# Layer norm scaling of a two-layer transformer-like kernel: two of four tiles moved from VectorE to GpSimd

## The chip, the cores and the metric

One NeuronCore of a Trainium2 chip runs the whole program in one launch. The time is device microseconds from the start to the end of an execution. The engines are TensorE (PE, matmuls and transposes), VectorE (DVE), ScalarE (ACT), GpSimd (POOL) and SyncE (SP, which only issues DMAs). Each works through its own queue strictly in order, and they meet at semaphores.

## What is computed

The input is x, 8 sequences of 1024 tokens with 256 features, in float32. Six blocks follow each other, each on a layer norm of x and each added back to x:

```python
x = x + 0.5 * L0_ffn(layernorm(x))    # token-shift mix, gate, squared relu, sigmoid
x = x + L0_attn(layernorm(x))         # linear attention, 16 heads of 16, chunked
x = x + 0.5 * L0_ffn(layernorm(x))
x = x + 0.5 * L1_ffn(layernorm(x))    # dense layer + one of four low-rank experts per token
x = x + L1_attn(layernorm(x))         # causal softmax attention with rotary embedding
x = x + 0.5 * L1_ffn(layernorm(x))

def layernorm(x):
    m, v = mean(x), var(x)            # over the 256 features
    return (x - m) / sqrt(v + 1e-5)
```

## The kernel before

The kernel is written engine by engine, with its own semaphores and no scheduler. A batch (one sequence) is cut into two halves of 512 tokens, and a half into four tiles of 128 tokens; a tile is 128 partitions by 256 features. The first five blocks of a half up to the rotated queries and keys are the front stream (`front_*`, halves 0 and 1). The softmax attention of all batches is the core stream (`core_*`: scores for the row maxima, L750; scores transposed, L765; exponent on ScalarE, L1310; causal select on GpSimd, L1458; values, L784). The output projection and the last block are the tail stream (`tail_*`, q = 2 and 3).

`weave` sets the order of the work. It counts 1166 ticks. In each tick every engine's code takes one step of the core stream and one step of each live generator, and a `yield` ends a step. The front of batch b starts at tick 120 b + 4 (half 0) and 120 b + 26 (half 1). Four engines run the same ticks; only VectorE's core stream lags by one. So the order on an engine is fixed by where the yields stand, and there is no clock: an engine that is held lets its whole queue wait.

Each norm has the same steps, and q tells half and stream:

- VectorE, tick 0: `bn_stats` (L819) and `bn_aggr` (L822), four each, into `mv`; semaphore `ln`.
- GpSimd, tick 1: variance plus epsilon (L1327), then to the power -0.5 (L1329) into `rstd`; semaphore `rs`.
- VectorE, tick 2: four `tensor_scalar` (L828), one per tile, (x - mean) * rstd into the buffer `dst`; semaphore `xn`.
- TensorE, tick 3: waits for four counts of `xn`, then eight transposes (L497) into two banks.
- ScalarE, tick 4: copies them to `xnT` (L1129), which the block's matmuls read.

There are 96 such norms: 5 x 2 x 8 in the front, 2 x 8 in the tail. The next batch's input overwrites x only when `xn` has reached 20 per batch, i.e. when all five norms of a half have been scaled.

GpSimd's other work stands in the same queue: the causal selects (L1458, 512), the shifted mix of the first block (L1341), the heads spread for linear attention (L1361), values by the key norm (L1369), masks (L1376), state sums (L1389), the rotary sum (L1432), and the router's root (L1413, L1415). On VectorE the core stream has the row maxima (L1104 with a mask, L1107 without), which free the two score banks that L750 fills.

Of the kernel before, what the change touches and what calls it, by code (L numbers as in the profile page):

```python
# [12 lines left out]
ALU = mybir.AluOpType  # L13
# [11 lines left out]
NC = T // CH  # L25
# [31 lines left out]
def macaron(nc, a, out):  # L57
    ctx = ExitStack()
    with ctx:
# [41 lines left out]
        mv = sb("mv", [P, 2 * NC, 4, 2])  # L101
# [318 lines left out]
        def idle(n):  # L420
            for _ in range(n):
                yield

        if True:

            with nc.Block() as block:
# [38 lines left out]
                def xq(q):  # L465
                    return x[:, 4 * q:4 * q + 4] if q < NC else xt[:, q - NC]
# [348 lines left out]
                def ln_dve(q, b, n, dst, ready):  # L815
                    xs = xq(q)
                    ready()
                    for t in range(4):
                        nc.vector.bn_stats(stats[:, q, t], xs[:, t]).then_inc(s["ln"][q], 1)  # L819
                    nc.vector.wait_ge(s["ln"][q], 8 * norms(q, b, n) + 4)  # L820
                    for t in range(4):
                        nc.vector.bn_aggr(mv[:, q, t], stats[:, q, t]).then_inc(s["ln"][q], 1)  # L822
                    yield
                    yield
                    nc.vector.wait_ge(s["ln"][q], 8 * norms(q, b, n) + 8)
                    nc.vector.wait_ge(s["rs"][q], 2 * norms(q, b, n) + 2)
                    for t in range(4):
                        nc.vector.tensor_scalar(dst[:, t], xs[:, t], mv[:, q, t, 0:1], rstd[:, q, t:t + 1], ALU.subtract,  # L828
                                                ALU.mult).then_inc(s["xn"][q], 1)
                    yield  # L830
                    yield
                    yield
# [488 lines left out]

                def ln_pool(q, b, n):
                    yield
                    nc.gpsimd.wait_ge(s["ln"][q], 8 * norms(q, b, n) + 8)
                    nc.gpsimd.tensor_scalar(varep[:, q], mv[:, q, :, 1], EPS, None, ALU.add).then_inc(s["rs"][q], 1)  # L1327
                    nc.gpsimd.wait_ge(s["rs"][q], 2 * norms(q, b, n) + 1)
                    nc.gpsimd.tensor_tensor(rstd[:, q], varep[:, q], mhalf[:], ALU.pow).then_inc(s["rs"][q], 1)  # L1329
                    yield  # L1330
                    yield from idle(3)

                def ffn_pool(c, b, f):
                    yield from ln_pool(c, b, 2 * f)
                    xT_ready(nc.gpsimd, c, b, 2 * f)
                    if b and f == 0 and c == 0:
                        nc.gpsimd.wait_ge(s["vout"][1], 16 * b)
                    if c:
                        nc.gpsimd.wait_ge(s["carry"], 2 * b + f + 1)
                    for k in range(KT):  # L1340
                        nc.gpsimd.tensor_scalar(xmB[:, :, k], xnT[c][:, k, PAD - 1:PAD - 1 + CH].rearrange("p (h t) -> p h t", h=2),  # L1341
                                                mu[:, 1, 1, k:k + 1], zcol[:], ALU.mult, ALU.add).then_inc(s["mixr"][c], 1)
                    yield
                    yield from idle(8)

                def lin_pool(c, b):
                    yield from ln_pool(c, b, 1)
                    if c == 0:
                        nc.gpsimd.memset(vlin[:, :, :, DK:2 * DK], 0.0).then_inc(s["lz"], 1)
                    yield from idle(7)  # L1350

                    def spread_heads(j):
                        if c == 0 and j == 0 and b >= 3:
                            f_filled(nc.gpsimd, 3, b - 3, "up", 1)
                        if j == 0:
                            for m in range(KT):
                                f_gone(nc.gpsimd, c, b, "q", m)
                        if j >= 2:
                            f_filled(nc.gpsimd, c, b, "sc", j - 2, 3)
                        for o in range(2):  # L1360
                            nc.gpsimd.tensor_scalar(qbd[:, j % 2, :, o], qT[:, :, j * P:(j + 1) * P], pmask[:, o:o + 1], zcol[:],  # L1361
                                                    ALU.mult, ALU.add).then_inc(s["qbd"][c], 1)

                    def scaled(j):
                        if j == 0:
                            nc.gpsimd.wait_ge(s["newton"][c], NEWTON * b + NEWTON)
                        f_gone(nc.gpsimd, c, b, "kv", j)
                        v = vlin[:, j].rearrange("p q (s d) -> p q s d", d=DK)[:, :, 0:3:2]
                        nc.gpsimd.tensor_tensor(v, v, krs[:, j].rearrange("p (q s) -> p q s", s=2).unsqueeze(3).broadcast_to([P, H // 2, 2, DK]),  # L1369
                                                ALU.mult).then_inc(s["vs"][c], 1)  # L1370

                    def select(j):
                        for i in (2, 3):
                            f_gone(nc.gpsimd, c, b, "sc", j, i)
                            v = scm[:, i].rearrange("p (j c) -> p j c", j=G)
                            nc.gpsimd.affine_select(out=v, in_=v, compare_op=ALU.is_ge, fill=0.0, base=0, pattern=[[0, G], [1, P]],  # L1376
                                                    channel_multiplier=-1).then_inc(s["sel"][c], 1)

                    def state(j):
                        t = 4 * c + j  # L1380
                        if t == 0 or t == NT - 1:
                            return
                        f_gone(nc.gpsimd, c, b, "st", j)
                        if t >= 2:
                            nc.gpsimd.wait_ge(s["st"], 6 * b + t - 1)
                            f_filled(nc.gpsimd, (t - 1) // 4, b, "y", (t - 1) % 4)
                        else:
                            f_gone(nc.gpsimd, 0, b, "st", 0)
                        nc.gpsimd.tensor_tensor(ssb[:, t % 2], ssb[:, (t - 1) % 2], smask, ALU.add).then_inc(s["st"], 1)  # L1389

                    spread_heads(0)
                    yield
                    spread_heads(1)
                    yield
                    for j in range(4):
                        if j == 0:
                            for i in range(4):
                                scaled(i)
                        if j in (1, 2):
                            spread_heads(j + 1)  # L1400
                        yield
                        yield
                        select(j)
                        state(j)
                        yield
                    yield from idle(4)

                def exp_pool(q, b, n):
                    e = 1 if q == 3 else 0
                    yield from ln_pool(q, b, n)  # L1410
                    yield from idle(4)
                    nc.gpsimd.wait_ge(s["es"][q], 17 * b + 3)
                    nc.gpsimd.tensor_scalar(narrow[:, e, 0], narrow[:, e, 0], 1e-24, None, ALU.max).then_inc(s["ep"][q], 1)  # L1413
                    nc.gpsimd.wait_ge(s["ep"][q], 2 * b + 1)
                    nc.gpsimd.tensor_tensor(narrow[:, e, 1], narrow[:, e, 0], mhalf[:], ALU.pow).then_inc(s["ep"][q], 1)  # L1415
                    yield
                    yield from idle(8)

                def qkv_pool(c, b):
                    yield from ln_pool(c, b, 4)  # L1420
                    yield
                    if c == 0:
                        nc.gpsimd.wait_ge(s["xu"][1], 4 * b + 4)
                        nc.gpsimd.memset(vst[:, :, :, DK:VP], 1.0).then_inc(s["vone"][0], 1)
                    yield
                    yield

                    def add(qk):
                        nc.gpsimd.wait_ge(s["rab"][c], 4 * b + 2 * qk + 2)
                        for m in range(KT):  # L1430
                            f_gone(nc.gpsimd, c, b, "qk", qk, m)
                        nc.gpsimd.tensor_tensor(ra, ra, rb, ALU.add).then_inc(s["rr"][c], 1)  # L1432

                    add(0)
                    yield
                    yield from idle(3)
                    add(1)
                    yield
                    yield from idle(2)
# [163 lines left out]
```

## Time and profile before

| | us |
|---|---|
| median of 3 runs | 2963.05 |
| lowest, highest | 2957.84, 2965.12 |
| the profiled execution | 2963.63 |
| its span | 2961.9 |

The span runs from the first to the last instruction of the profiled execution; its own time holds another 1.7 us around it. Busy time doesn't count instructions that only wait or issue DMAs. A timeline row gives start, length, engine, line and how many instructions are merged in it; in brackets is the idle time ahead of it and what ended that. `arena` is the name of one large buffer in which many tiles lie; `bank` is PSUM.

### The profile page before, as it was taken

Reading aid. Unit: us, or ns where it says so; the run is one execution under the profiler, and the core shown is the slowest. Engines: PE = TensorE matmul, PEld = TensorE weight load, DVE = VectorE, ACT = ScalarE, POOL = GpSimd, SP = SyncE. Lnnn points to the kernel's source line nnn. Section 1 sums busy time; section 2 is a strip of 40 time slices with the busy share of each in tenths; the row PEclk is TensorE's granted clock in tenths of the full one; section 3 lists DMA queues with packets and bytes.
Section 4 is the critical chain, followed back from the end, with each engine's and each line's share of the span. In section 5 each row is a group of like instructions: output and inputs, shape, how many; then the busy total and the mean of one; then the engine's idle time right before and its main releaser. Section 6 shows DMA issues by size and latency. Waiting matters only on the chain.

```text
span 2961.9 us, 45503 instructions
## 1 busy us (share of the span) xinstructions
PE 2640.6 (89%) x15278; PEld 1740.0 (59%) x15278; DVE 1862.2 (63%) x5534; ACT 1230.0 (42%) x2802; POOL 754.6 (25%) x1283
## 2 busy tenths in 40 slices
PE   4885899899999999899999999989998999998986
PEld 3563666456655666466665666556664666555644
DVE  5544667666677567666667666675676666766642
ACT  1321244444444444444444444444444444444452
POOL 2321232223222232223322232222322233211111
PEclk8996899989999999999999899999999999999998
DMA  2015103411333113411134113331134121443211
GB/s 59 1 46 134 23 17 80 115 41 25 70 91 98 39 41 82 129 49 45 38 96 123 40 27 68 93 95 45 35 78 123 52 52 23 100 119 76 64 38 47
DMA packets 137423, 193.97 MB, mean 65 GB/s; under 512 B 49439, under 2 KB 111214, under 8 KB 127854
## 3 DMA queue, kind: packets, MB, share of 16 engines
q1 hardware_dynamic: 131808, 190.89, 25.9%
q8 instruction: 129, 2.11, 0.3%
q10 hardware_dynamic: 5390, 0.18, 0.1%
q14 instruction: 96, 0.79, 0.1%
HBM read 122.34 MB, written 67.63 MB: 64 GB/s over the span
## 4 chain that ended last, share of the span: by engine, by line
PE 71%; DVE 16%; DMA 4%; issue 3%; ACT 3%; POOL 2%; SPq 1%; DVEq 0%; ACTq 0%; POOLq 0%
PE bank L765 9%; PE bank L784 9%; PE bank L750 8%; PE bank L587 5%; PE bank L678 4%; PE bank L518 4%; PE bank L567 4%; PE bank L527 3%; PE bank L536 3%; PE bank L692 3%; DVE bank L1104 3%; PE bank L622 2%; PE bank L497 2%; PE bank L633 2%; PE bank L561 2%
## 5 line engine op out<-in xcount | busy, mean ns | idle before, releaser
L1310 ACT ACTIVATE pexp<-bank 128x512 f32<-128x512 f32 (+3 forms) x1536 | 675.8, 497 | 555.1 <-PE bank L765 554.9
L1104 DVE CUSTOM_DVE_ANT_0 bank<-bank,maskneg 128x256 f32<-128x256 f32 (+3 forms) x1024 | 484.9, 511 | 294.1 <-PE bank L750 291.5
L765 PE MATMUL bank<-stq,stk 128*128 128x512 f32 (+3 forms) x1536 | 558.6, 435 | 58.0 <-ACT pexp L1310 54.9
L750 PE MATMUL bank<-stk,stq 128*128 128x512 f32 (+3 forms) x1536 | 512.8, 399 | 100.1 <-DMA stk<-k_halves 31.3
L765 PEld LDWEIGHTS bank<-stq,stk 128*128 128x128 f32 x1536 | 274.5, 200 | 344.3 <-ACT pexp L1310 210.4
L1107 DVE TENSOR_REDUCE mxa<-bank 128x1 f32<-128x512 f32 x512 | 348.7, 685 | 133.2 <-PE bank L750 128.4
L1458 POOL TENSOR_SCALAR_AFFINE_SELECT pexp<-pexp 128x256 f32<-128x256 f32 x512 | 214.3, 425 | 743.0 <-ACT pexp L1310 742.6
L750 PEld LDWEIGHTS bank<-stk,stq 128*128 128x128 f32 x1536 | 288.2, 203 | 184.5 <-issue 120.6
L784 PE MATMUL bank<-pexp,vsm 128*32 128x512 f32 (+3 forms) x3072 | 360.9, 544 | 5.7 <-POOL pexp L1458 5.5
L1376 POOL TENSOR_SCALAR_AFFINE_SELECT arena<-arena 128x512 f32<-128x512 f32 x128 | 78.5, 638 | 416.3 <-ACT arena L1212 416.3
L587 PE MATMUL bank<-arena 32*128 32x256 f32 x1024 | 158.0, 428 | 17.2 <-DVE arena L911 14.2
L1327 POOL TENSOR_SCALAR varep<-mv 128x4 f32<-128x4 f32 x96 | 22.6, 235 | 488.6 <-DVE mv L822 488.6
L1129 ACT COPY xnT<-bank 128x512 f32<-128x512 f32 x160 | 88.8, 602 | 140.3 <-PE bank L497 140.1
L518 PE MATMUL bank<-arena,wk 128*128 128x256 f32 x512 | 141.0, 425 | 6.5 <-DVE arena L852 6.4
L497 PE MATMUL bank<-ident,arena 128*128 128x128 f32 x768 | 119.4, 306 | 30.7 <-DVE arena L828 29.9
L587 PEld LDWEIGHTS bank<-arena 32*128 32x128 f32 x1024 | 95.2, 198 | 69.8 <-issue 51.7
L497 PEld LDWEIGHTS bank<-ident,arena 128*128 128x128 f32 x768 | 101.3, 159 | 54.5 <-DVE arena L828 34.7
L1432 POOL TENSOR_TENSOR arena<-arena 128x1024 f32<-128x1024 f32 x32 | 75.8, 2368 | 224.1 <-DVE arena L1026 224.1
L784 PEld LDWEIGHTS bank<-pexp,vsm 128*32 128x32 f32 x3072 | 63.5, 112 | 117.5 <-issue 89.8
L911 DVE TENSOR_TENSOR arena<-bank,mask 128x512 f32<-128x512 f32 x128 | 82.2, 683 | 77.0 <-PE bank L587 77.0
L518 PEld LDWEIGHTS bank<-arena,wk 128*128 128x128 f32 x512 | 108.3, 217 | 37.5 <-DVE arena L852 10.8
L1150 ACT ACTIVATE arena<-bank 128x512 f32<-128x512 f32 x64 | 38.3, 598 | 207.0 <-PE bank L518 207.0
(186 smaller groups left out, 4204.3 us busy)
## 6 DMA issues: line engine op xcount, KB each, us to landing
stq<-q_halves SPq DMA_DIRECT2D x128, 256.0 KB
arena<-rope_table SPq DMA_DIRECT2D x8, 2048.0 KB
q_halves<-arena SPq DMA_DIRECT2D x32, 512.0 KB, 3.0
k_halves<-arena SPq DMA_DIRECT2D x32, 512.0 KB, 2.8
stk<-k_halves SPq DMA_DIRECT2D x64, 256.0 KB
stk<-k_halves SPq DMA_DIRECT2D x128, 128.0 KB
v_rows<-arena SPq DMA_DIRECT2D x16, 544.0 KB, 4.1
vsm<-v_rows SPq DMA_DIRECT2D x16, 544.0 KB, 3.8
```

Of the source, the lines that this page charges most:

```text
L497: last = nc.tensor.transpose(bk[:, t * P:(t + 1) * P], src[:, t, k * P:(k + 1) * P], ident[:])
L518: last = mm(bk[:, m * D:(m + 1) * D], wk0[:, k, m * P:(m + 1) * P], xmA[:, h, k], start=k == 0, stop=k == KT - 1)
L567: last = mm(bk, xn[:, k, j * P:(j + 1) * P], wqkv[:, k, D:3 * D], start=k == 0, stop=k == KT - 1)
L587: last = mm(bks[i][:, k * D:(k + 1) * D], khT[rows, k, j * P:(j + 1) * P], qbd[rows, j % 2, k], start=k == 0, stop=k == KT - 1, skip_group ...
L678: mm(bk[:, i * D:(i + 1) * D], xn[:, k, t * P:(t + 1) * P], wf1[:, k], start=k == 0, stop=False)
L750: last = mm(bk[:, col:col + n], stq[b_][:, h % 2, qb * P:(qb + 1) * P], stk[b_][:, h % 2, k0:k0 + n], start=True, stop=True)
L765: mm(ps(j)[:, 0:n], stk[b_][:, j, kb * P:(kb + 1) * P], stq[b_][:, j, (c + 1) * CH - n:(c + 1) * CH], start=True, stop=True).then_inc(s["t ...
L784: last = mm(ps(2)[HP * j:HP * (j + 1), CH - n:CH], vsm[:, kb, at:at + HP], pexp[:, (u - 1 + j // 2) % NPX, j % 2, 0:n], start=kb == 0, sto ...
L1104: last = nc.vector.tensor_tensor_reduce(out=sc, in0=sc, in1=maskneg[:, CH - n:CH], scale=1.0, scalar=LOWEST, op0=ALU.add, op1=ALU.max, acc ...
L1107: last = nc.vector.reduce_max(dst, sc, AX)
L1310: nc.scalar.activation(pexp[:, u % NPX, j, 0:n], ps(j)[:, 0:n], ACT.Exp, scale=DK ** -0.5).then_inc(s["exp_done"], 1)
L1458: nc.gpsimd.affine_select(out=v, in_=v, compare_op=ALU.is_ge, fill=0.0, base=0, pattern=[[0, 2], [1, P]], channel_multiplier=-1).then_inc( ...
```

## The change

In `ln_dve` VectorE scales tiles 0 and 1 only. In `ln_pool` GpSimd, which has just computed the root, takes the next tick's step too. It waits for its own root (`rs`) and for the first count of `xn` of this norm, that is, for the end of VectorE's scaling of tile 0, and then scales tiles 2 and 3 into the same buffer with the same operands. Each scaling still adds one to `xn`, so that TensorE waits for the same four counts. The callers pass the buffer.

```diff
--- before.py
+++ after.py
@@ -824,7 +824,7 @@
                     yield
                     nc.vector.wait_ge(s["ln"][q], 8 * norms(q, b, n) + 8)
                     nc.vector.wait_ge(s["rs"][q], 2 * norms(q, b, n) + 2)
-                    for t in range(4):
+                    for t in range(2):
                         nc.vector.tensor_scalar(dst[:, t], xs[:, t], mv[:, q, t, 0:1], rstd[:, q, t:t + 1], ALU.subtract,
                                                 ALU.mult).then_inc(s["xn"][q], 1)
                     yield
@@ -1321,17 +1321,23 @@
 
 
 
-                def ln_pool(q, b, n):
+                def ln_pool(q, b, n, dst):
+                    xs = xq(q)
                     yield
                     nc.gpsimd.wait_ge(s["ln"][q], 8 * norms(q, b, n) + 8)
                     nc.gpsimd.tensor_scalar(varep[:, q], mv[:, q, :, 1], EPS, None, ALU.add).then_inc(s["rs"][q], 1)
                     nc.gpsimd.wait_ge(s["rs"][q], 2 * norms(q, b, n) + 1)
                     nc.gpsimd.tensor_tensor(rstd[:, q], varep[:, q], mhalf[:], ALU.pow).then_inc(s["rs"][q], 1)
                     yield
+                    nc.gpsimd.wait_ge(s["rs"][q], 2 * norms(q, b, n) + 2)
+                    nc.gpsimd.wait_ge(s["xn"][q], 4 * norms(q, b, n) + 1)
+                    for t in (2, 3):
+                        nc.gpsimd.tensor_scalar(dst[:, t], xs[:, t], mv[:, q, t, 0:1], rstd[:, q, t:t + 1], ALU.subtract,
+                                                ALU.mult).then_inc(s["xn"][q], 1)
                     yield from idle(3)
 
                 def ffn_pool(c, b, f):
-                    yield from ln_pool(c, b, 2 * f)
+                    yield from ln_pool(c, b, 2 * f, xns)
                     xT_ready(nc.gpsimd, c, b, 2 * f)
                     if b and f == 0 and c == 0:
                         nc.gpsimd.wait_ge(s["vout"][1], 16 * b)
@@ -1344,7 +1350,7 @@
                     yield from idle(8)
 
                 def lin_pool(c, b):
-                    yield from ln_pool(c, b, 1)
+                    yield from ln_pool(c, b, 1, xns)
                     if c == 0:
                         nc.gpsimd.memset(vlin[:, :, :, DK:2 * DK], 0.0).then_inc(s["lz"], 1)
                     yield from idle(7)
@@ -1407,7 +1413,7 @@
 
                 def exp_pool(q, b, n):
                     e = 1 if q == 3 else 0
-                    yield from ln_pool(q, b, n)
+                    yield from ln_pool(q, b, n, xns if q < NC else xnsG[q - NC])
                     yield from idle(4)
                     nc.gpsimd.wait_ge(s["es"][q], 17 * b + 3)
                     nc.gpsimd.tensor_scalar(narrow[:, e, 0], narrow[:, e, 0], 1e-24, None, ALU.max).then_inc(s["ep"][q], 1)
@@ -1417,7 +1423,7 @@
                     yield from idle(8)
 
                 def qkv_pool(c, b):
-                    yield from ln_pool(c, b, 4)
+                    yield from ln_pool(c, b, 4, xnsq)
                     yield
                     if c == 0:
                         nc.gpsimd.wait_ge(s["xu"][1], 4 * b + 4)
```

(Lines of GpSimd behind the edit stand six higher in the changed kernel: L1458 becomes L1464.)

VectorE's queue keeps its order. It is shown where two norms stand close together, which is some 1280 us into the program, where both halves' tail norms follow each other. Before:

```order
L1104 ISA mxb 128x1
L828 TENSOR_SCALAR arena<-arena,mv,rstd 128x256 x4
L819 BN_STATS stats<-arena 128x6 x4
L822 BN_AGGR mv<-stats 128x2 x4
L1104 ISA bank,mxa<-bank,maskneg 128x128
```

Now:

```order
L1104 ISA mxb 128x1
L828 TENSOR_SCALAR arena<-arena,mv,rstd 128x256 x2
L819 BN_STATS stats<-arena 128x6 x4
L822 BN_AGGR mv<-stats 128x2 x4
L1104 ISA bank,mxa<-bank,maskneg 128x128
```

Only the count of L828 differs, there and in the other 95 norms.

GpSimd's queue at the same place, over both norms. The roots are L1327 and L1329 (now L1328 and L1330), the causal selects L1458 (now L1464), the router's root L1413 (now L1419). Before:

```order
L1327 TENSOR_SCALAR varep<-mv 128x4
L1329 TENSOR_TENSOR rstd<-varep,mhalf 128x4
L1458 AFFINE_SELECT pexp<-pexp 128x2x128
L1327 TENSOR_SCALAR varep<-mv 128x4
L1329 TENSOR_TENSOR rstd<-varep,mhalf 128x4
L1458 AFFINE_SELECT pexp<-pexp 128x2x128 x5
L1413 TENSOR_SCALAR narrow<-narrow 128x4
```

Now:

```order
L1328 TENSOR_SCALAR varep<-mv 128x4
L1330 TENSOR_TENSOR rstd<-varep,mhalf 128x4
L1335 TENSOR_SCALAR arena<-arena,mv,rstd 128x256 x2
L1464 AFFINE_SELECT pexp<-pexp 128x2x128
L1328 TENSOR_SCALAR varep<-mv 128x4
L1330 TENSOR_TENSOR rstd<-varep,mhalf 128x4
L1464 AFFINE_SELECT pexp<-pexp 128x2x128
L1335 TENSOR_SCALAR arena<-arena,mv,rstd 128x256 x2
L1464 AFFINE_SELECT pexp<-pexp 128x2x128 x4
L1419 TENSOR_SCALAR narrow<-narrow 128x4
```

The new pair L1335 stands directly behind the root in the first norm, ahead of a select that followed the root before; in the second norm one of the five selects comes between.

## Rows read from the trace of the kernel before

**Rows 1.** The page: busy time of each engine, and the chain by engine.
```profile
PE 2640.6 (89%) x15278; PEld 1740.0 (59%) x15278; DVE 1862.2 (63%) x5534; ACT 1230.0 (42%) x2802; POOL 754.6 (25%) x1283
...
PE 71%; DVE 16%; DMA 4%; issue 3%; ACT 3%; POOL 2%; SPq 1%; DVEq 0%; ACTq 0%; POOLq 0%
```

**Rows 2.** Windows of start, steady part and end: engines, clock, DMA.
```profile
core 0: us, PE busy (x) PEld busy (x) DVE busy (x) ACT busy (x) POOL busy (x), PEclk, DMA share, GB/s
...
372.00:2560.00 2188.00, 2041.18 (x12098) 1346.45 (x12091) 1443.32 (x4317) 969.89 (x2220) 585.80 (x995) 0.95 0.27 66
```

**Rows 3.** Waits of TensorE: who waited for whom, total, times, longest.
```profile
PE bank L497 <- DVE arena L828: 29.9, 11, 6.8
PE bank L750 <- DVE mxa L1104: 29.9, 30, 2.3
...
PE bank L784 <- POOL pexp L1458: 5.5, 8, 0.7
```

**Rows 4.** Groups by line and shape on VectorE and GpSimd.
```profile
L828 DVE TENSOR_SCALAR arena<-x,mv,rstd 128x256 f32<-128x256 f32 x320 | 116.6, 426 | 8.7 <-POOL rstd L1329 8.4
...
L828 DVE TENSOR_SCALAR arena<-arena,mv,rstd 128x256 f32<-128x256 f32 x64 | 23.3, 424 | 6.4 <-POOL rstd L1329 6.4
...
L1361 POOL TENSOR_SCALAR arena<-arena,pmask,zcol 128x256 f32<-128x256 f32 x128 | 72.5, 577 | 54.4 <-PE bank L679 48.9 <-ACT arena L1183 5.5
L1369 POOL TENSOR_TENSOR arena<-arena,krs 128x256 f32<-128x256 f32 x64 | 52.9, 857 | 28.8 <-DVE krs L884 28.8
```

**Rows 5.** Timeline of the first norm (start, us, engine, what).
```profile
39.15 1.05 POOL L1329 TENSOR_TENSOR rstd<-varep,mhalf 128x4 f32<-128x4 f32 x1
40.30 1.38 DVE L828 TENSOR_SCALAR arena<-x,mv,rstd 128x256 f32<-128x256 f32 x4 [1.57 <-POOL rstd L1329]
...
41.74 1.97 PE L497 MATMUL bank<-ident,arena 128*128 128x128 f32 x8 [6.84 <-DVE arena L828]
```

**Rows 6.** Timeline: two norms close together, 1275 to 1287 us.
```profile
1275.66 0.68 POOL L1458 TENSOR_SCALAR_AFFINE_SELECT pexp<-pexp 128x256 f32<-128x256 f32 x1
...
1279.94 1.37 DVE L828 TENSOR_SCALAR arena<-arena,mv,rstd 128x256 f32<-128x256 f32 x4
...
1281.34 0.43 PE L784 MATMUL bank<-pexp,vsm 128*32 128x128 f32 x8
...
1281.70 1.09 PE L497 MATMUL bank<-ident,arena 128*128 128x128 f32 x8
...
1284.61 1.55 DVE L828 TENSOR_SCALAR arena<-arena,mv,rstd 128x256 f32<-128x256 f32 x4 [0.80 <-POOL rstd L1329]
...
1286.08 0.68 DVE L1104 CUSTOM_DVE_ANT_0 bank<-bank,maskneg 128x512 f32<-128x512 f32 x1
...
1286.97 0.47 PE L750 MATMUL bank<-stk,stq 128*128 128x512 f32 x1 [1.28 <-DVE mxa L1104]
```

**Rows 7.** Timeline: norms before router work and 1.49 us before transposes.
```profile
1134.03 1.50 DVE L828 TENSOR_SCALAR arena<-x,mv,rstd 128x256 f32<-128x256 f32 x4
...
1137.03 1.27 PE L497 MATMUL bank<-ident,arena 128*128 128x128 f32 x5
...
1305.45 1.47 DVE L828 TENSOR_SCALAR arena<-x,mv,rstd 128x256 f32<-128x256 f32 x4
...
1306.97 1.97 PE L497 MATMUL bank<-ident,arena 128*128 128x128 f32 x8 [0.47 <-DVE arena L828]
...
1311.77 0.99 PE L765 MATMUL bank<-stq,stk 128*128 128x512 f32 x2 [0.56 <-ACT pexp L1310]
```

**Rows 8.** Timeline: first and last stalls behind a scaling and VectorE work.
```profile
331.06 0.47 PE L750 MATMUL bank<-stk,stq 128*128 128x512 f32 x1 [1.23 <-DVE mxa L1104]
...
2668.59 0.47 PE L750 MATMUL bank<-stk,stq 128*128 128x512 f32 x1 [2.27 <-DVE mxa L1104]
```

**Rows 9.** Timeline: GpSimd's two-pointer scale alone, and over L828.
```profile
1012.71 1.10 POOL L1361 TENSOR_SCALAR arena<-arena,pmask,zcol 128x256 f32<-128x256 f32 x2
...
1065.38 1.30 POOL L1361 TENSOR_SCALAR arena<-arena,pmask,zcol 128x256 f32<-128x256 f32 x2
```

## The prediction

> **What bounds the kernel now.** I read the page first, for the load of the engines and for the chain of work that ended last. TensorE is busy 89% of the span and carries 71% of the chain; VectorE is busy 63% and carries 16%; GpSimd is busy 25% and carries 2% [rows 1]. The windows then show that the long middle, 372 to 2560 us, has TensorE at 2041 of 2188 us, with a granted clock of 0.95 [rows 2]. So the kernel is near the limit of one engine. A change elsewhere can win only those waits of TensorE that its engine ends, and lose only where it makes new ones.
>
> The view of TensorE's waits names them. It waited 29.9 us in 11 places for a scaling (L828) itself, and 29.9 us in its score matmuls for the maximum on VectorE (L1104), whose bank was not free; for GpSimd's causal select (L1458) it waited 5.5 us in all [rows 3]. The two VectorE waits pull this change in opposite directions. The first wants the four scaled tiles soon. The second wants VectorE free soon.
>
> **The change, part by part.** VectorE loses two of four L828 in each of 96 norms: 192 of 384 instructions, whose groups hold 116.6 + 23.3 us of busy time [rows 4]. Four together took 1.38 us on a quiet engine [rows 5], at about 0.41 us for one and a start every 0.32 us; two take 0.73. VectorE is thus free 0.65 us earlier, 96 times, or 62 us in all (3% of its busy time). Its statistics and the root on GpSimd are not touched.
>
> GpSimd gains 192 scalings. No row shows one there. The nearest is L1361: the same kind of instruction, two per-partition operands, 256 elements, one input from SBUF. Two of them took 1.10 us alone and 1.30 us while a scaling ran on VectorE [rows 9]. From below I take two at 0.41 each as VectorE does them, 0.8 us. From above I take L1369, 256 elements from two tensors, 857 ns each [rows 4], so 1.7 us. I use 1.2 us, between the two readings of L1361, because VectorE's second scaling will overlap the start of GpSimd's first.
>
> **When the four tiles are ready.** GpSimd waits until VectorE's first scaling has ended. In the first norm the root ended at 40.20 and VectorE started at 40.30 [rows 5], so a wait across engines costs 0.1 us. The new end is 0.41 + 0.1 + 1.2 = 1.71 us after VectorE's start, where it was 1.38: 0.33 us later (bounds: 0.07 earlier at 0.8 us a pair, 0.83 later at 1.7). I set the end of the fourth scaling against the first transpose for all 96 norms. In 16 the transpose starts within 0.2 us: the eleven waits of [rows 3] and five near them, mostly at the start (40.30, then 41.74, [rows 5]) and at the end, and one per batch as at 1305.45, then 1306.97 [rows 7]. There the delay is paid: 16 x 0.33 = **5.3 us lost**. One more per batch has 0.38 us of slack (1279.94 + 1.37, then 1281.70, [rows 6]) and just covers it. The other norms of the steady part have more than half a microsecond, most of them more than one (1134.03 + 1.50, then 1137.03, [rows 7]).
>
> **What VectorE's relief is worth.** I followed the chain in stretches of 60 us and looked at what stands behind each L828 on it. In 24 places more VectorE work comes first and then a wait of TensorE, the first at 331.06 (apart from one in the start-up) with 1.23 us, the last but one at 2668.59 with 2.27 us [rows 8]. These waits sum to about 25 us, but each can shrink only by 0.65 us, or twice that where two norms follow each other, or by all of itself. That gives some 18 us. Five of the pairs look like [rows 6]: L828 at 1279.94, statistics, root, L828 at 1284.61, L1104 at 1286.08, TensorE after 1.28 us of waiting at 1286.97. The same five and one near the end lose something on the other side, below: about 5 us. That leaves 13 us. TensorE arrives earlier at its next wait and gives some of it back, since 147 us of the steady window are still idle [rows 2]; I take three quarters, **10 us won**.
>
> **What stands behind the new wait on GpSimd.** It works in order. Today it finishes the root and goes on to the next selects while VectorE is still microseconds away from its scaling (the select at 1275.66, the scaling at 1279.94, [rows 6]); now it stops there. Behind the waiting instruction stand the causal selects, which TensorE's value matmuls (L784) wait for. For each select I compared its new start (old start, or the end of GpSimd's pair) with the L784 that needs it: 59 needed ones are late, by 0.4 to 7.7 us, but nearly all have more slack than that. Six do not. Five are of the kind in [rows 6]: the select that ran at 1275.66 is now held until the pair is done at 1281.6, ends at 1282.0, and the L784 that stood at 1281.34 starts some 0.75 us late. The sixth costs 1.5. This is the 5 us already taken off. The root of a following norm never comes late: at 1283 GpSimd has been free for a microsecond. Selects, masks and head spreads that VectorE, ScalarE or TensorE need otherwise are held by less than their slack.
>
> A rule that speaks against the change: VectorE's scaling reads one tensor, yet four of them took 1.55 us beside selects at 1284.61 and 1.37 us without [rows 6], and GpSimd's pair 1.30 instead of 1.10 [rows 9]. So the two engines do hold each other up. The Trainium skill (SBUF — State Buffer, Who interferes with whom) has them share one pair of ports as an exclusive lock, and exempts a one-input VectorE instruction outside its two-port modes; the lock is borne out here, the exemption isn't. With a full lock GpSimd's first scaling would start only when VectorE's second has ended, at 0.73 us rather than 0.51, and the loss at the 16 transposes would be 16 x 0.45 = 7 us in place of 5.3.
>
> **The sum.** 2963.6 (this execution) + 5.3 - 10 = 2959. The median of the runs shown is 0.6 us below the profiled execution, so 2958.5.
>
> **Rivals.** What a measurement of this kernel can tell from no change is about 0.3%, or 9 us.
>
> (a) Forecast: loss and gain nearly cancel, 2954 to 2972 us. For it: 93% of the steady part is matmul time that nothing here touches, and both terms are small. Chance 0.54.
>
> (b) The relief goes through in full. 18 us come off, the late selects cost nothing because TensorE itself arrives later there, and stalls behind other VectorE work shrink too. 2963 - 18 + 5 = 2950, perhaps 2944. For it: VectorE has 16% of the chain [rows 1]. Against it: VectorE's queue runs dry often, and where it does, being early is worth nothing. Chance 0.27.
>
> (c) Slower: GpSimd's scaling is dear. The place is the transposes. At 0.857 us each (L1369's price) the tiles are 0.83 us late: 16 x 0.83 = 13.3 at the tight transposes, 5 x 0.45 = 2.2 at those with 0.38 us of slack, 6 x 0.6 = 3.6 more for late selects, against the 10 won: 2963 + 19 - 10 = 2972. From a pair of 1.7 us upwards it decides; at 2.2 us, where norms with 1.3 us of slack come in as well, it is 2985 or more. Against it: L1361 at 577 ns in the mean of 128, busy VectorE included [rows 4]. Chance 0.19, which includes a queue on GpSimd that jams more often than my comparison says. The Trainium skill (GPSIMD Engine Reference, Key points) says that "for elementwise work, the DVE is structurally ~2× faster", that is some 0.8 us for one scaling; its table in Engine selection calls one-input work roughly line-rate, and L1361 sides with that.
>
> **Range.** Low 2943 takes in (b). High 2976 takes in the threshold case of (c); beyond it I leave 0.08, below it 0.06. The likeliest case by itself is 2954 to 2972. Chances: faster by over 0.3% 0.27, within it 0.54, slower 0.19.
>
> **What would show it.** L828 at 192 instructions, 0.73 us a pair, and near 70 us busy. The new GpSimd line at 0.56 to 0.65 us each, near 115 us busy, so GpSimd at 29%. TensorE's wait for scaling (now on GpSimd) up from 29.9 us by about 5; its waits on L1104 and L1107 down by about 10; its wait on the select up from 5.5 to some 10. TensorE's busy time is unchanged within 2 us at the same clock. I am wrong if the new line takes over 0.8 us, if TensorE waits for selects more than 15 us, or if the waits on the score maxima fall by 20 us.

## The result, and the profile after

| | before | after |
|---|---|---|
| median, us | 2964.09 (4 runs) | 2999.16 (4 runs) |
| lowest, highest | 2957.84, 2968.92 | 2984.51, 3001.8 |
| the profiled execution | 2963.63 | 3001.8 |

The ratio is 1.0109 with an interval of 1.0071 to 1.0147. The changed kernel is 35 us slower, and the time lies outside the predicted 2943 to 2976. The cause had a place among the rivals, as (c), but the price was far beyond the one that I worked with.

The page of the changed kernel, busy time and the chain by engine:

```profile
PE 2646.7 (88%) x15278; PEld 1746.7 (58%) x15278; DVE 1800.0 (60%) x5342; ACT 1232.6 (41%) x2802; POOL 980.8 (33%) x1475
...
PE 58%; DVE 11%; POOL 3%; issue 3%; DMA 2%; ACT 2%; SPq 1%; DVEq 0%; POOLq 0%; ACTq 0%
```

VectorE lost 62 us, as computed [rows 1]. GpSimd gained 226 us, where I had put 115. TensorE's busy time rose by 6.1 us and the span by 38.1, so 32 us of the rise are time in which TensorE isn't busy. The shares of the two chains can't be compared: before they add up to 100% of the span, here to 80%, since this one is followed back only to some 600 us. The waits of TensorE say where the idle time is:

```profile
PE bank L497 <- POOL arena L1335: 65.4, 32, 8.5
...
PE bank L750 <- DVE mxa L1107: 25.9, 29, 3.1
...
PE bank L587 <- DVE arena L911: 20.9, 20, 3.2
PE bank L784 <- POOL pexp L1464: 19.2, 14, 3.3
PE bank L750 <- DVE mxa L1104: 15.8, 20, 1.4
PE bank L750 <- DVE mxb L1104: 14.9, 31, 2.1
```

Three of these rows of the kernel before, beside those in [rows 3]:

```profile
PE bank L750 <- DVE mxa L1107: 25.7, 29, 2.8
...
PE bank L587 <- DVE arena L911: 14.2, 14, 2.6
...
PE bank L750 <- DVE mxb L1104: 11.2, 29, 1.2
```

The wait for scalings went from 29.9 to 65.4 us and that for selects from 5.5 to 19.2; the linear attention's masked scores (L911) cost 6.7 us more. The score matmuls wait for the row maxima in three rows, which fell together from 66.8 to 56.6 us, so by the 10 us that were predicted. The largest of them alone (29.9 to 15.8) would say more than that. The groups by line and shape on both engines name the reason:

```profile
L1335 POOL TENSOR_SCALAR arena<-x,mv,rstd 128x256 f32<-128x256 f32 x160 | 196.3, 1233 | 197.1 <-DVE arena L828 197.1
L1335 POOL TENSOR_SCALAR arena<-arena,mv,rstd 128x256 f32<-128x256 f32 x32 | 39.2, 1233 | 32.6 <-DVE arena L828 32.6
...
L828 DVE TENSOR_SCALAR arena<-x,mv,rstd 128x256 f32<-128x256 f32 x160 | 58.5, 408 | 7.8 <-POOL rstd L1330 7.6
```

One scaling on GpSimd takes 1233 ns. I had taken 600 for half a pair, and 850 as the upper bound. The 230 us behind the second bar, over 96 norms, are GpSimd idle until VectorE's first scaling has ended, with its own queue held up behind it. The timeline of the first norm, to be laid beside [rows 5]:

```profile
39.22 1.05 POOL L1330 TENSOR_TENSOR rstd<-varep,mhalf 128x4 f32<-128x4 f32 x1
40.38 0.73 DVE L828 TENSOR_SCALAR arena<-x,mv,rstd 128x256 f32<-128x256 f32 x2 [1.57 <-POOL rstd L1330]
40.98 2.45 POOL L1335 TENSOR_SCALAR arena<-x,mv,rstd 128x256 f32<-128x256 f32 x2 [0.71 <-DVE arena L828]
...
43.49 1.33 PE L497 MATMUL bank<-ident,arena 128*128 128x128 f32 x5 [8.52 <-POOL arena L1335]
```

Everything around the pair is nearly as computed: VectorE's two take 0.73 us, and GpSimd starts 0.60 us behind VectorE, where 0.51 was computed. But the pair takes 2.45 us, so the tiles are ready 3.05 us behind VectorE's start instead of 1.38. In all 96 norms it is 3.03 to 3.09 us. I set the end of the pair against the transpose again: now 38 norms are tight (within 0.2 us), where 16 were before. The eleventh norm's transposes, in the changed kernel:

```profile
302.25 1.97 PE L497 MATMUL bank<-ident,arena 128*128 128x128 f32 x8 [2.05 <-POOL arena L1335]
```

and the same ones in the kernel before:

```profile
285.97 1.97 PE L497 MATMUL bank<-ident,arena 128*128 128x128 f32 x8 [0.38 <-DVE arena L828]
```

That is 16.3 us of delay within the first 300 us, where one stream runs alone and nothing lies behind a norm to fill the gap. At the 34th norm (962 us) it is 24.6 us behind, at the 58th (1648 us) 31.4, at the last (2935 us) 35.9.

### The profile page after: what moved, and what is told of

Same layout as the page of the kernel before. It is cut to its first block, busy times and chain, and to the rows that moved or that the text cites. A ratio compares the mean times of both kernels' runs of the same rounds, so it can differ in the third digit from the quotient of the medians.

```text
span 3000.0 us, 45599 instructions
## 1 busy us (share of the span) xinstructions
PE 2646.7 (88%) x15278; PEld 1746.7 (58%) x15278; DVE 1800.0 (60%) x5342; ACT 1232.6 (41%) x2802; POOL 980.8 (33%) x1475
## 4 chain that ended last, share of the span: by engine, by line
PE 58%; DVE 11%; POOL 3%; issue 3%; DMA 2%; ACT 2%; SPq 1%; DVEq 0%; POOLq 0%; ACTq 0%
PE bank L765 8%; PE bank L784 8%; PE bank L750 6%; PE bank L678 3%; PE bank L587 3%; PE bank L527 3%; PE bank L567 3%; PE bank L536 3%; PE bank L692 2%; PE bank L497 2%; PE bank L518 2%; DVE bank L1104 2%; POOL arena L1335 2%; PE bank L679 2%; PE bank L622 2%
## 5 line engine op out<-in xcount | busy, mean ns | idle before, releaser
L1464 POOL TENSOR_SCALAR_AFFINE_SELECT pexp<-pexp 128x256 f32<-128x256 f32 x512 | 209.9, 416 | 629.4 <-ACT pexp L1310 628.8
L784 PE MATMUL bank<-pexp,vsm 128*32 128x512 f32 (+3 forms) x3072 | 359.7, 543 | 19.5 <-POOL pexp L1464 19.2
L1335 POOL TENSOR_SCALAR arena<-x,mv,rstd 128x256 f32<-128x256 f32 x160 | 196.3, 1233 | 197.1 <-DVE arena L828 197.1
L497 PE MATMUL bank<-ident,arena 128*128 128x128 f32 x768 | 125.5, 316 | 65.5 <-POOL arena L1335 65.4
L1328 POOL TENSOR_SCALAR varep<-mv 128x4 f32<-128x4 f32 x96 | 22.8, 237 | 394.4 <-DVE mv L822 394.4
L911 DVE TENSOR_TENSOR arena<-bank,mask 128x512 f32<-128x512 f32 x128 | 82.2, 684 | 82.4 <-PE bank L587 82.2
```

The costliest lines, as they stand in the source:

```text
L497: last = nc.tensor.transpose(bk[:, t * P:(t + 1) * P], src[:, t, k * P:(k + 1) * P], ident[:])
L784: last = mm(ps(2)[HP * j:HP * (j + 1), CH - n:CH], vsm[:, kb, at:at + HP], pexp[:, (u - 1 + j // 2) % NPX, j % 2, 0:n], start=kb == 0, sto ...
L1335: nc.gpsimd.tensor_scalar(dst[:, t], xs[:, t], mv[:, q, t, 0:1], rstd[:, q, t:t + 1], ALU.subtract, ALU.mult).then_inc(s["xn"][q], 1)
```

## The experiments

Ratios are against the kernel before, run beside each; intervals are 95%.

**What does GpSimd pay for?** A copy of the kernel before, in which GpSimd runs several forms of the instruction twice each at the start, while it has nothing else to do.

```diff
+                forms = ((ALU.subtract, ALU.mult, pa, pb, D), (ALU.mult, ALU.add, pa, pb, D), (ALU.mult, ALU.subtract, pa, pb, D),
+                         (ALU.add, ALU.mult, pa, pb, D), (ALU.subtract, ALU.mult, 1.0, 2.0, D), (ALU.subtract, ALU.mult, pa, pb, P),
+                         (ALU.mult, ALU.mult, pa, pb, D))
+                for i, (o0, o1, s0, s1, w) in enumerate(forms):
+                    for j in range(2):
+                        nc.gpsimd.tensor_scalar(xb[:, 2 + 2 * i + j, 0:w], xb[:, 0, 0:w], s0, s1, o0, o1)
+                nc.gpsimd.tensor_scalar(xb[:, 16], xb[:, 0], pa, None, ALU.subtract)
```

> The kernel before, with eight forms of GpSimd's one-input instruction run twice each on 128 partitions in its idle start-up time, on spare buffers: subtract and mult with two per-partition operands (the changed kernel's form, 1233 ns there), mult and add (the form of L1361), mult and subtract, add and mult, subtract and mult with two constants, subtract and mult over 128 elements, mult and mult, and subtract alone. Theory A (the pair of operations sets the price): mult and add takes about 560 ns, subtract and mult 1230 ns; the others show which forms are cheap. Theory B (the shape or the place sets it: L1361 reads rows of 128 elements, or the scaling collides with VectorE): mult and add takes 1230 ns as well here, or subtract and mult drops to 560 ns in the quiet start-up. The time of the whole says nothing.

The timeline of GpSimd, the first of subtract-mult, one of mult-add, one of mult-subtract, one of add-mult, and the subtraction alone:

```profile
14.59 1.24 POOL L245 TENSOR_SCALAR arena<-arena,mv,rstd 128x256 f32<-128x256 f32 x1
...
17.02 0.56 POOL L245 TENSOR_SCALAR arena<-arena,mv,rstd 128x256 f32<-128x256 f32 x1
...
18.09 1.23 POOL L245 TENSOR_SCALAR arena<-arena,mv,rstd 128x256 f32<-128x256 f32 x1
...
20.50 0.56 POOL L245 TENSOR_SCALAR arena<-arena,mv,rstd 128x256 f32<-128x256 f32 x1
...
26.45 0.93 POOL L246 TENSOR_SCALAR arena<-arena,mv 128x256 f32<-128x256 f32 x1
```

Every form that has a subtraction is dear, every form without one is cheap, in the same shape and from the same operands, within 14 us of each other. In the changed kernel the shortest of the 192 took 1215 ns and the longest 1284, so work beside it isn't the reason either. Theory A holds. With constants in place of the pointers subtract-mult still takes 1082 to 1110 ns, on 128 elements 795. My reference row, L1361, is a mult-add.

**The change with the cheap form.** The same queue, waits and tiles, but GpSimd multiplies and adds (the expectation says what its tiles hold).

```diff
-                        nc.gpsimd.tensor_scalar(dst[:, t], xs[:, t], mv[:, q, t, 0:1], rstd[:, q, t:t + 1], ALU.subtract,
-                                                ALU.mult).then_inc(s["xn"][q], 1)
+                        nc.gpsimd.tensor_scalar(dst[:, t], xs[:, t], rstd[:, q, t:t + 1], mv[:, q, t, 0:1], ALU.mult,
+                                                ALU.add).then_inc(s["xn"][q], 1)
```

> The changed kernel, but GpSimd's two scalings use mult and add with the same operands in the other order (x times root plus mean), so tiles 2 and 3 do not hold the norm. Theory A: the instruction takes about 560 ns, the pair ends 1.7 us behind VectorE's start instead of 3.04, and the time falls from 2999 to 2955 to 2968, which is what the prediction gave for that price. Theory B (shape or collision): it stays at 1230 ns and 2999 us. Theory C (GpSimd's waiting in its queue is what costs, not the length of the instruction): the instruction gets short but the time stays above 2985.

It took 2950.42 us, 0.9945 [0.9929, 0.9961]. Its group and TensorE's waits:

```profile
L1335 POOL TENSOR_SCALAR arena<-x,rstd,mv 128x256 f32<-128x256 f32 x160 | 89.0, 564 | 193.2 <-DVE arena L828 193.2
```

```profile
PE bank L497 <- POOL arena L1335: 34.4, 15, 7.2
...
PE bank L784 <- POOL pexp L1464: 11.2, 14, 1.9
```

The tiles are ready at 1.69 to 1.71 us, the 1.71 of the prediction; the wait for scalings rose by 4.5 us, where 5.3 was computed. The pair of operations is worth 49 us and turns the sign of the change. The time lies 5 us below the expected 2955 to 2968: the kernel is some 16 us faster than before, where the terms of the prediction gave 5.

**VectorE's relief alone.** VectorE scales two tiles, nobody the other two (the ready tiles are transposed twice).

```diff
-                            last = nc.tensor.transpose(bk[:, t * P:(t + 1) * P], src[:, t, k * P:(k + 1) * P], ident[:])
+                            last = nc.tensor.transpose(bk[:, t * P:(t + 1) * P], src[:, t % 2, k * P:(k + 1) * P], ident[:])
...
-                    for t in range(4):
+                    for t in range(2):
...
-                                                ALU.mult).then_inc(s["xn"][q], 1)
+                                                ALU.mult).then_inc(s["xn"][q], 2)
```

> The kernel before, but VectorE scales tiles 0 and 1 only and nobody tiles 2 and 3; TensorE transposes tiles 0 and 1 twice, so half of each norm is left out. GpSimd is as before. It measures the term won: VectorE 0.65 us earlier in 96 norms, tiles ready 0.65 us earlier too. The prediction's term: 10 us won behind the scaling, and here another 16 x 0.65 = 10 at the tight transposes, so 2944. A rival: the relief is worth next to nothing apart from the tight transposes: 2953.

It took 2920.89 us, 0.9848 [0.9821, 0.9874], 45 us faster, and so below both values of the expectation. I had put the relief at 10 with the tiles no earlier. So either the earlier tiles bring a lot, or the relief was under-priced. The next one separates them.

**Early tiles without relief.** VectorE scales all four; TensorE transposes tiles 0 and 1 twice, and waits for two counts instead of four.

```diff
-                    nc.tensor.wait_ge(s["xn"][q], 4 * norms(q, b, n) + 4)
+                    nc.tensor.wait_ge(s["xn"][q], 4 * norms(q, b, n) + 2)
```

> The kernel before, but TensorE transposes tiles 0 and 1 twice and waits only for these two, while VectorE still scales four (two waits of ScalarE and VectorE keep later writers behind the scaling; they are long met). It is the run that gave 45 us less, without the relief: tiles 0.65 us earlier and VectorE as loaded as before. Half of each norm is left out. By the prediction's count 16 x 0.65 = 10 us, 2955. If it gives 20 us or more, the tight transposes are more than I counted; the rest of the 45 us is relief.

It took 2967.45 us, 1.0019 [1.0, 1.0037]. The wait for scalings fell by 5 us and that for maxima rose by about as much (29.9 to 34.4). Early tiles alone bring nothing, where the expectation had 10 us. What the relief brings needs VectorE's shorter queue.

**One tile only.** VectorE scales three, GpSimd the fourth, with its subtraction.

```diff
-                    for t in range(2):
+                    for t in range(3):
...
-                    for t in (2, 3):
+                    for t in (3,):
```

> VectorE scales three tiles, GpSimd only the last, behind VectorE's first as in the change. At 1.23 us the tile is ready at 0.6 + 1.23 = 1.83 us behind VectorE's start, where it was 1.38 (before) and 3.04 (changed). If the time of readiness sets the cost: 0.45 of 1.66 us late is about a quarter of the 36 us, less the smaller relief of 0.32 us: 2967 to 2973. If GpSimd's waiting behind VectorE is what costs, it stays near 2990, since the wait is the same.

It took 2949.26 us, 0.9934 [0.9918, 0.9949], 18 us below the nearer of the two expectations. One dear instruction (1405 ns beside VectorE's other two scalings) is bearable, two are not: readiness is 1.98 to 2.06 us, the wait for scalings 39.1 us, for selects 12.9.

**The queue load alone.** VectorE scales all four tiles. GpSimd takes the change's two waits and then four small instructions of as much time, which write four numbers to a place that nothing reads.

```diff
+                    nc.gpsimd.wait_ge(s["rs"][q], 2 * norms(q, b, n) + 2)
+                    nc.gpsimd.wait_ge(s["xn"][q], 4 * norms(q, b, n) + 1)
+                    idle_out = xnT[1][:, 0, 0:4]
+                    for o in range(4):
...
+                        if o in (0, 2):
+                            last = nc.gpsimd.tensor_tensor(idle_out, varep[:, q], mhalf[:], ALU.pow)
+                        else:
+                            last = nc.gpsimd.tensor_scalar(idle_out, varep[:, q], EPS, None, ALU.add)
```

> VectorE scales all four tiles as before and TensorE waits for these alone; GpSimd takes the change's two waits and is then busy with four small instructions on a spare corner (two roots, two additions, each behind the last, some 2.7 us) instead of two scalings. The queue on GpSimd is the only thing left of the change: no relief for VectorE, no late tiles, no large tensor on the shared side. If late selects cost what the changed kernel's waits say (19.2 us against 5.5 for L784), 2978 to 2985 beside 2965. If they hide, within 5 us of the kernel before.

It took 3005.25 us, 1.0136 [1.0115, 1.0156], 20 us above the upper end of the expectation, although no tile is later than before. VectorE isn't relieved here. The waits of TensorE, to be laid beside [rows 3]:

```profile
PE bank L497 <- DVE arena L828: 31.5, 13, 6.8
...
PE bank L784 <- POOL pexp L1478: 30.8, 20, 3.6
...
PE bank L615 <- POOL arena L1396: 11.4, 16, 2.2
```

The wait for scalings stays where it was. The wait for selects is 25 us longer and that for the masks of the linear attention (L615, 3.1 before) 8 longer. The load ends 3.36 us behind VectorE's start, in seven norms 3.88, which is later than the change's pair at 3.05, and TensorE waits longer for selects than in the change (30.8 us against 19.2). So the 41 us are an upper estimate of what the queue costs in the change.

**The load, and TensorE waits for it.** The last of the four counts for the tiles too, so that they are late as well.

```diff
-                    nc.tensor.wait_ge(s["xn"][q], 4 * norms(q, b, n) + 4)
+                    nc.tensor.wait_ge(s["xn"][q], 5 * norms(q, b, n) + 5)
```

> As the run before, but TensorE's transposes also wait for the last of GpSimd's four small instructions, about 3.3 us behind VectorE's start (3.04 in the changed kernel). It is the change without its relief. If lateness is what costs, it is the slowest of all: the changed kernel's 2999 plus what the relief is worth, which the run with VectorE alone put at up to 45 us, so 3020 to 3045. If the relief is worth only the 10 us of the prediction, 3005 to 3015.

It took 3019.22 us, 1.0191 [1.0169, 1.0213], at the lower end of what was expected if lateness costs. Lateness adds 14 us to the load, and the place differs. By the transposes' start, this kernel is 14.9 us behind the kernel before at the eleventh norm, the load alone 5.1; at the 22nd it is 20.2 and 1.2, and from the 34th on the two lose almost in step (28.3 and 4.1 there, 56.9 and 39.9 us at the last norm). Late tiles without the load weren't tried.

**The wait alone, and half the load.** The first takes the two waits and nothing behind them; the second the waits and two of the four small instructions.

```diff
-                    for o in range(4):
+                    for o in range(2):
```

> VectorE scales four tiles; GpSimd takes the change's two waits (its own root, VectorE's first scaling) and then does nothing. It tells the wait from the work behind it in the run with 3.4 us of load, which was 41 us slower than before. If the wait alone holds the selects too long, 10 us or more remain, 2973 and up. If it is the wait plus the length of the work (slack of the selects used up only by both), it is within 5 us of the kernel before.

> As the load run, with only one root and one addition (about 1.35 us) behind the wait, so that GpSimd is free some 1.9 us behind VectorE's start, as late as in the run with the cheap pair (1.70). If slack is used up at a threshold, nearly all 41 us go: 2965 to 2975. If each late microsecond costs the same, about half stays: 2985.

They took 2960.78 us, 0.9982 [0.9963, 1.0001], and 2958.61 us, 0.9976 [0.9956, 0.9997]. The wait, for which I had feared the selects, costs nothing, and 1.35 us of work behind it costs nothing either; 2.7 us of work cost 41. Half the load makes TensorE wait 12.7 us for selects, 7 more than before, and none of it reaches the end. So it does no harm that GpSimd is held until 1.9 us behind VectorE's start, and until 3.4 us it does; where between them the harm begins wasn't measured.

The half load shows one thing more. Its waits for the maxima, with VectorE scaling all four tiles:

```profile
PE bank L750 <- DVE mxa L1107: 26.0, 30, 2.8
...
PE bank L750 <- DVE mxa L1104: 16.6, 23, 1.4
...
PE bank L750 <- DVE mxb L1104: 12.2, 30, 2.0
```

Together they are 54.8 us, 12 less than before and less than in the change, though VectorE isn't relieved at all. So the 10 us by which they fell in the change are no measure of the relief: TensorE, when it is held elsewhere, seems to wait less for the maxima.

**The whole computation in the cheap form.** GpSimd turns the sign of the four means (one instruction on 128x4) and then adds and multiplies; once with two tiles, once with the last one only.

```diff
+                    nc.gpsimd.tensor_scalar(varep[:, q], mv[:, q, :, 0], -1.0, None, ALU.mult).then_inc(s["rs"][q], 1)
...
-                        nc.gpsimd.tensor_scalar(dst[:, t], xs[:, t], mv[:, q, t, 0:1], rstd[:, q, t:t + 1], ALU.subtract,
+                        nc.gpsimd.tensor_scalar(dst[:, t], xs[:, t], varep[:, q, t:t + 1], rstd[:, q, t:t + 1], ALU.add,
```

> The full computation: GpSimd first negates the four means (one small instruction behind its root, while VectorE does its first scaling) and then scales tiles 2 and 3 as (x plus negated mean) times root, add and mult. From the table of forms each takes 562 ns. If the pair of operations is all that made the change slow, this gives the time of the run with mult and add, 2950 beside 2968, i.e. 0.5% to 0.6% under the kernel before.

> As the run before, but GpSimd takes only tile 3 and VectorE three. Ready at 0.6 + 0.6 to 0.75, which is 1.2 to 1.35 us behind VectorE's start, no later than before; relief 0.32 us a norm instead of 0.65. If lateness at tight transposes weighs more than relief, it beats the two-tile form: 2940 to 2948. If relief weighs more, it is behind it: 2952 to 2960.

They took 2953.18 us, 0.9961 [0.9945, 0.9978], and 2948.79 us, 0.9955 [0.9938, 0.9971]. Both beat both kernels. The one-tile form lies between the two cases of its expectation and decides between neither. The negation takes 273 ns and in 82 of the 96 norms lies in the time in which GpSimd waits for VectorE anyway; in 14 it starts the pair up to 0.3 us later. With one tile, the plain subtraction (0.9934) is as good as the sum form: the intervals overlap.

## Why the prediction was wrong

**The price of GpSimd's pair.** This is the step that failed: "The nearest is L1361: the same kind of instruction". It was the same in shape, type and number of operands, and not in its operations. I took 1.2 us with 1.7 as the upper bound; it measured 2.46. The time of readiness follows from there: with 2.46 us it is 0.41 + 0.1 + 2.46 = 2.97 us after VectorE's start, against a measured 3.03 to 3.09. With the cheap form 1.71 was computed and 1.69 to 1.71 came, in part by luck, since GpSimd started 0.1 us later and its pair took 0.1 us less than I had put; 5.3 us of waits for scalings were computed and 4.5 came. The time doesn't follow: the sum gave 5 us less than before, and the cheap form brought 16. The price explains the sign; the gain was too small too, as is shown below.

**The bound "from above".** L1369, a product of two tensors at 857 ns, was no bound at all: an instruction with one tensor input cost 1233. The Trainium skill's line that I weighed (GPSIMD Engine Reference, Key points, VectorE "structurally ~2× faster") fits neither form: 1233 to 408 ns is a factor of 3, 564 to 408 one of 1.4. Its table in Engine selection, one-input work at roughly line rate, comes near only for the forms without a subtraction. So the L1361 row decided between two statements for the wrong instruction.

**Rival (c)** had the right cause, with "at 2.2 us 2985 or more", and in the transposes one of its places; late selects were a small term there. The pair is 2.46 and the time 2999. I had written that the prediction was wrong if the new line took over 0.8 us; it did. What drove the low chance of 0.19 was the same wrong row.

**GpSimd's queue behind the wait.** "Six do not" have slack, 5 us in all. With the cheap form TensorE's wait for selects rose by 5.7 us (to 11.2), so the count held for the pair that I had assumed. With the dear pair the wait for selects is 19.2 us, above the 15 that the prediction named as a sign of being wrong, and a load a little longer than the pair costs 41 us by itself. The wait alone, which had worried me most, costs nothing. The cost doesn't grow in proportion; at 1.35 us of work it is nil. In the load's kernel the loss begins late: 4.1 us at the 34th norm (962 us), 24.4 at the 58th (1648 us), 34.0 at the 82nd (2346 us), that is, when front, core and tail all run. In the change itself the course is another: 16.3 us are lost by the eleventh norm and 24.6 by the 34th, and only 11 more from there to the last. So most of the change's loss lies where the load alone costs little (5.1 and 4.1 us at the same norms).

**The relief of VectorE.** "10 us won" was near for the waits and wrong for the time. With half the scalings left out, the three rows of waits for the maxima fell by 7.7 us together (to 59.1) and those for scalings by 5.5. The time fell by 45. Busy and idle time of TensorE in the profiled executions show where the rest is:

| kernel | span | TensorE busy | rest of the span |
|---|---|---|---|
| before | 2961.9 | 2640.6 | 321.3 |
| change | 3000.0 | 2646.7 | 353.3 |
| mult-add form | 2946.3 | 2629.3 | 317.0 |
| relief alone | 2924.8 | 2611.2 | 313.6 |
| one tile | 2941.4 | 2612.1 | 329.3 |
| load alone | 3004.1 | 2657.1 | 347.0 |
| load and late | 3021.1 | 2653.1 | 368.0 |

The relief with the earlier tiles took 7.7 us of idle time away, where 20 was expected of both, and 29.4 us of busy time, with the same 15278 matmuls. The mean granted clock is 0.940 in place of 0.930. These lines are the means over the run, before and then relief alone:

```profile
core 0: 2961.9 us, clock 0.930
```

```profile
core 0: 2924.8 us, clock 0.940
```

The clock isn't all of it. Five of the six executions had 0.940 to 0.946 and took 2915 to 2927 us; the sixth, at 0.930, took 2940. The kernel before's seven executions at 0.930, over all rounds, took 2960 to 2971. So some 25 us of the 45 seem to remain at an equal clock, an estimate that rests on one execution.

The step that failed here is the count of the relief in waits alone, with "TensorE's busy time is unchanged within 2 us at the same clock". In the change busy time rose by 6 us, at 0.925, against the idle time's 32, which is thus most of the loss.

**The two engines beside each other.** The full lock that the prediction weighed doesn't show. In the change GpSimd's pair starts at 0.60 us, before VectorE's second scaling has ended (0.73), and takes 2.45 us, as the two alone do (1236 and 1222 ns). They do slow each other elsewhere: in the one-tile kernels, with a third scaling of VectorE beside it, GpSimd's subtraction takes 1405 ns in place of 1233, and the sum form a median of 732 in place of 558. That "the exemption isn't" borne out isn't shown: no row tells in which mode VectorE's scaling runs.

**The sum, as the runs split it.** Load and lateness together cost 56 us, the change 35. The difference of some 20 us would be what VectorE's relief gives in the change; alone it gave 45. The parts don't add, and the load's kernel holds GpSimd 0.3 us longer per norm than the change does, so this split is an estimate, and probably too high for the relief.

**What stays open.** How much of the change's 35 us is late tiles and how much is the queue on GpSimd. Why the relief is worth 45 us alone and some 20 under load: part of it goes with the granted clock, and which of the waits that went had stood ahead of a fall of the clock wasn't traced. The one-tile kernel's profiled execution (2943.2 us) gained 28.5 us of busy time and lost 8 of idle time, and its median is 6 us above that execution. Whether its gain is a matter of which falls it happens to miss, I can't say. GpSimd's scaling without its wait for VectorE's first scaling wasn't tried, since the wait keeps the use of the buffer in order.

## What to carry to other kernels

Price an instruction on GpSimd by a row with the same operations, not only the same shape: here add-mult for subtract-mult, with the sign turned in a tiny instruction ahead, moved the time from +1.1% to -0.4%. Where work goes into an in-order queue, the price isn't the wait but the length of what stands behind the release against the slack of what is queued: here nothing when GpSimd was free 1.9 us behind VectorE's start, 41 us when it was 3.4. A shorter wait in one row isn't a gain until the time says so: the waits for the maxima fell without any relief. And where TensorE is near its limit, a wait saved or made is counted at its own length only as a first term: look at its busy time at an equal number of matmuls too, and at the granted clock, which was 0.940 with the relief and 0.930 without.

## What the runs showed of the hardware

**The subtraction on GpSimd.** On 128x256 float32: 1222 to 1236 ns with a subtraction in either place and two pointers, 557 to 563 with mult-add, add-mult and mult-mult, 927 to 934 for a subtraction alone. The power on 128x4 takes 1043 ns, more than a subtraction on 64 times as many elements.

**The granted clock after a gap.** In the kernel before, TensorE's score matmul at 1688.43 had waited 2.16 us for ScalarE's exponent:

```profile
1688.43 0.98 PE L765 MATMUL bank<-stq,stk 128*128 128x512 f32 x2 [2.16 <-ACT pexp L1310]
```

The windows around it, from the start of the gap on:

```profile
1686.00:1690.00 4.00, 1.84 (x9) 0.89 (x9) 3.59 (x15) 3.76 (x7) 1.30 (x3) 1.00 0.00 0
1690.00:1700.00 10.00, 10.00 (x38) 5.73 (x35) 7.78 (x13) 2.06 (x5) 6.55 (x11) 0.50 0.21 57
```

TensorE ran at 2.4 GHz (1.00), was idle for half of 4 us, and then worked for 10 us without a gap at 1.2 GHz (0.50), which by these rows is up to 5 us of work lost behind a wait of 2.16 (an estimate: half of ten). Of the 219 slices of 10 us between 370 and 2560 us, 48 have a granted clock below 0.9 in the kernel before, 35 with the relief alone, 35 with one tile, 47 in the change and 50 with the load. So a wait can cost more than its own length, and a relief that shortens waits can bring more than they last; that it does so here is argued from these counts and not shown by a run. They don't follow the time in every kernel: the change, 35 us slower, has no more low slices than the kernel before.
